# Row maxima moved by ScalarE from PSUM into the query stack, the first layer's mask added by TensorE, and two phases in a new order

## What is computed

```python
logits = q @ k.T * scale            # per head: 512 x 512; the first layer adds a Fourier bias
logits = where(causal, logits, -inf)
attn = softmax(logits)              # exp(logits - row maximum) / sum
out = attn @ v
```

## Time and profile before

| | us |
|---|---|
| median of three runs | 4009.02 |
| the profiled execution, its own time | 3993.08 |
| its span in the profile | 3991.3 |
| PE busy | 3393.3 (85%) |
| DVE busy | 2720.8 (68%) |
| ACT busy | 2003.3 (50%) |
| POOL busy | 1021.1 (26%) |
| mean granted clock of TensorE | 0.923 |

### The profile page before, as it was taken

How to read it: one execution, slowest core, us unless ns; L and a number is a source line. 1 busy time by engine, 2 the same in 40 slices (tenths; PEclk the granted TensorE clock), 3 DMA queues, 4 the chain that set the end, 5 groups by cost and what they waited for, 6 DMA issues and landing times.

```text
span 3991.3 us, 58259 instructions
## 1 busy us (share of the span) xinstructions
PE 3393.3 (85%) x19406; PEld 2516.8 (63%) x19406; DVE 2720.8 (68%) x8320; ACT 2003.3 (50%) x3683; POOL 1021.1 (26%) x1554
## 2 busy tenths in 40 slices
PE   2798888888888874789999999999999884799998
PEld 1566666666666652567777777777777653566665
DVE  5577777877877754356666667766666653588886
ACT  3355555555555542234444444444444443477776
POOL 1133433333433332112222222222222210000000
PEclk8899999999999986899999999999999976799999
DMA  6444444344444302134444444444444432000010
GB/s 180 68 84 85 74 77 80 76 91 80 75 76 79 63 16 74 32 74 70 84 86 86 85 86 85 84 82 84 82 84 86 75 70 85 1 32 32 32 32 22
DMA packets 207497, 284.23 MB, mean 71 GB/s; under 512 B 50977, under 2 KB 135970, under 8 KB 198370
## 3 DMA queue, kind: packets, MB, share of 16 engines
q1 hardware_dynamic: 207202, 280.52, 35.3%
HBM read 179.49 MB, written 96.73 MB: 69 GB/s over the span
## 4 chain that ended last, share of the span: by engine, by line
PE 63%; DMA 13%; DVE 9%; ACT 6%; issue 4%; POOL 3%; SPq 2%; POOLq 0%; ACTq 0%; DVEq 0%
PE ps L812 34%; DMA q_stack<-nmaxT 11%; PE ps L960 8%; PE ps L939 6%; PE ps L1158 5%; PE ps L974 4%; ACT pt L1623 2%; PE ps L914 2%; POOL pt L1812 1%; PE ps L985 1%; SPq L1937 1%; DVE ps L1304 1%; PE ps L1034 1%; DVE bn L1333 1%; DVE x_ring L1330 1%
## 5 line engine op out<-in xcount | busy, mean ns | idle before, releaser
L1304 DVE CUSTOM_DVE_ANT_0 ps<-ps,future 128x512 f32<-128x512 f32 (+3 forms) x2048 | 958.5, 514 | 335.4 <-PE ps L939 328.6
L1623 ACT ACTIVATE pt<-ps 128x512 f32<-128x512 f32 x1280 | 719.7, 597 | 513.4 <-PE ps L960 499.9
L960 PE MATMUL ps<-q_stack,k_stack 97*128 97x512 f32 (+3 forms) x2048 | 563.6, 355 | 214.7 <-DMA q_stack<-nmaxT 181.9
L1812 POOL TENSOR_SCALAR_AFFINE_SELECT pt<-pt 128x256 f32<-128x256 f32 x1024 | 404.9, 432 | 731.0 <-ACT pt L1623 730.8
L960 PEld LDWEIGHTS ps<-q_stack,k_stack 97*128 97x128 f32 x2048 | 365.7, 200 | 352.5 <-DMA q_stack<-nmaxT 214.2
L939 PE MATMUL ps<-k_stack,q_stack 96*128 96x512 f32 (+3 forms) x2048 | 540.0, 347 | 52.0 <-DVE nmax L1304 33.4
L939 PEld LDWEIGHTS ps<-k_stack,q_stack 96*128 96x128 f32 x2048 | 374.4, 203 | 130.4 <-issue 44.9
L974 PE MATMUL ps<-pt,v_ones 128*32 128x512 f32 (+3 forms) x4096 | 331.2, 468 | 34.0 <-POOL pt L1812 34.0
L1818 POOL TENSOR_TENSOR rs<-rs,mhalf 128x4 f32<-128x4 f32 x96 | 97.2, 1013 | 1024.7 <-DVE rs L1340 1024.7
L1834 POOL TENSOR_TENSOR hid<-hid,gate_of 128x512 f32<-128x512 f32 x128 | 164.3, 1283 | 690.4 <-DVE hid L1444 690.4
L812 PE MATMUL ps<-eh,w_hi 128*128 128x512 f32 (+1 forms) x672 | 282.1, 420 | 13.9 <-DVE xl L1285 11.4
(11 more groups left out here) (268 smaller groups left out, 7438.9 us busy)
## 6 DMA issues: line engine op xcount, KB each, us to landing
qk_scratch<-parts SPq DMA_DIRECT2D x64, 1024.0 KB, 5.5
q_stack<-qk_scratch SPq DMA_DIRECT2D x384, 128.0 KB, 5.0
k_stack<-qk_scratch SPq DMA_DIRECT2D x384, 128.0 KB, 5.7
gate_of<-gate_scratch SPq DMA_DIRECT2D x128, 256.0 KB, 5.0
x_mid<-x_ring SPq DMA_DIRECT2D x32, 512.0 KB, 2.6
x_ring<-x_mid SPq DMA_DIRECT2D x32, 512.0 KB, 4.9
x_ring<-in_x SPq DMA_DIRECT2D x16, 512.0 KB, 4.6
out_dram<-x_ring SPq DMA_DIRECT2D x16, 512.0 KB, 3.0
```

The costliest lines, as they stand in the source:

```text
L960: done = e.matmul(bank(bank_of[piece])[:, at:at + SEQ - j * P], a.k[0:97, base + h, j * P:(j + 1) * P], a.q[0:97, base + h, j * P:SEQ], st ...
L1304: done = e.tensor_tensor_reduce(src, src, future[:, SEQ - width:SEQ], -1.0, 3e38, ALU.add, ALU.min, nmax[:, g % 2, u // 5 * 2 + h, t:t + 1])
L1623: e.activation(dst, src, ACT.Exp).then_inc(exp_up.sem)
L1812: done = e.affine_select(out=blk, in_=blk, compare_op=ALU.is_ge, fill=0.0, base=0, pattern=[[0, 2], [1, P]], channel_multiplier=-1)
```

## The change

1. `N` is four transposes instead of one: one for each tile of 128 queries, of the 128x4 maxima of the four heads, side by side in the same bank as 4x512.
2. ScalarE's copy to `nmaxT`, `nmaxT` itself and the DMA `mr` are gone. ScalarE has pieces `mr` instead, two for each group, one for two heads each: two activations copy the bank's 4x512 into rows 96 to 99 of `q_stack` at the head's place, with scale -1 in the first layer.
3. Rows 96 to 99 of `k_stack` hold, for head h of a group, a one in row 96+h and zeros in the others. `T` runs over 100 rows and picks its head's row by that. `T`'s units 0 and 5 wait for the copies of their half.
4. `N`'s bank is left when the second `mr` is done (`leaves`).
5. First layer only: VectorE's custom instruction gives way to a plain maximum (`tensor_reduce`) without mask and negation, one for each product and one for both products of unit 4 and 9 of a group, 14 a group. The mask is added before by TensorE: behind each of the 16 score products one more product, bf16, identity 128x128 times the diagonal block of `future`, 128 columns, into the same place. The second layer keeps the custom instruction.
6. GpSimd's fill of row 96 becomes copies of the identity's corner into rows 96 to 99, in both prologues.
7. The due times of phases 1 and 2 are all new (period 74.24 to 71.3 in phase 1, 91.43 kept in phase 2), and with them the order on every engine. Phase 3's table is unchanged.

```diff
 TABLE = {
-    1: (74.24, {
+    1: (71.3, {
...
             put("N", n, g)
-            put("mr", n, g)
+            put("mr", n, g, 0)
+            put("mr", n, g, 1)
...
+            if kind == "N":
+                return max_row[key + (1,)], "scalar", ("mr",) + key + (1,)
...
                         done = e.matmul(bank(bank_of[piece])[:, at:at + width],
                                         a.q[0:96, base + h, t * P:(t + 1) * P], a.k[0:96, base + h, 0:width],
-                                        start=True, stop=True)
+                                        start=True, stop=a.layer == 1)
+                        if a.layer == 0:
+                            done = e.matmul(bank(bank_of[piece])[:, at + t * P:at + width], ident_b[:, :],
+                                            future[:, SEQ - P:SEQ], start=False, stop=True)
...
-                    e.transpose(bank(bank_of[piece])[0:GROUP * TT, 0:P], a.nmax[:, g % 2].rearrange("p h t -> p (h t)"),
-                                ident[:, :]).then_inc(nmax_up.sem)
+                    for t in range(TT):
+                        done = e.transpose(bank(bank_of[piece])[0:GROUP, t * P:(t + 1) * P], a.nmax[:, g % 2, :, t],
+                                           ident[:, :])
+                    done.then_inc(nmax_up.sem)
...
-                    if u == 0:
-                        e.wait_ge(*max_row[g % 2][n, g])
+                    if u % 5 == 0:
+                        e.wait_ge(*max_row[n, g, u // 5])
...
-                                        a.k[0:97, base + h, j * P:(j + 1) * P], a.q[0:97, base + h, j * P:SEQ],
+                                        a.k[0:100, base + h, j * P:(j + 1) * P], a.q[0:100, base + h, j * P:SEQ],
...
+                    if n < BATCH:
+                        first = u // 5 * 2
+                        if u % 5 == 4:
+                            done = e.tensor_reduce(nmax[:, g % 2, first:first + 2, 1],
+                                                   bank(bank_of[piece]).rearrange("p (h k) -> p h k", h=2), AX.X, ALU.max)
+                        else:
+                            for h, t, at in SCORES[u % 5]:
+                                done = e.tensor_reduce(nmax[:, g % 2, first + h, t:t + 1],
+                                                       bank(bank_of[piece])[:, at:at + (t + 1) * P], AX.X, ALU.max)
+                        done.then_inc(max_up.sem)
+                        continue
...
-                elif kind == "N":
-                    n, g = key
-                    before = group_before(n, g, 1)
-                    if before:
-                        e.wait_ge(*max_row[1 - g % 2][before])
-                    e.wait_ge(*nmax_up[key])
-                    e.activation(att[n // BATCH].nmaxT[:, :], bank(bank_of[piece])[0:GROUP * TT, 0:P],
-                                 ACT.Copy).then_inc(nmax_copy.sem)
+                elif kind == "mr":
+                    n, g, half = key
+                    a = att[n // BATCH]
+                    base = (g % a.sets) * GROUP + 2 * half
+                    if half == 0:
+                        e.wait_ge(*nmax_up[n, g])
+                    for h in range(2):
+                        done = e.activation(a.q[96:100, base + h, :], bank(bank_of["N", n, g])[0:GROUP, :], ACT.Copy,
+                                            scale=-1.0 if n < BATCH else 1.0)
+                    done.then_inc(max_row.sem)
...
-                    e.memset(att[1].k[96:97, :, :].bitcast(F32), 1.0).then_inc(consts.sem)
+                    for k in range(att[1].sets):
+                        done = e.tensor_copy(att[1].k[96:100, GROUP * k:GROUP * (k + 1), :],
+                                             ident[0:GROUP, 0:GROUP].unsqueeze(2).broadcast_to([GROUP, GROUP, SEQ]))
+                    done.then_inc(consts.sem)
...
-                elif kind == "mr":
-                    n, g = key
-                    a = att[n // BATCH]
-                    base = (g % a.sets) * GROUP
-                    e.wait_ge(*nmax_copy[key])
-                    e.dma_start(a.q[96:97, base:base + GROUP, :].bitcast(F32).rearrange("p h (t q) -> p (h t) q", q=P),
-                                a.nmaxT[:, :].bitcast(F32)).then_inc(max_row[g % 2].sem, 16)
```

More of the change, by code:

```diff
@@ L207 @@
         "tensor": {
[25 rows of a table removed]
[25 rows of a table added]
         },
         "scalar": {
[19 rows of a table removed]
[19 rows of a table added]
         },
         "vector": {
[18 rows of a table removed]
[18 rows of a table added]
         },
         "gpsimd": {
[L276 to L280 removed]
+            "tb a1": [109.964],
+            "sel": [174.864, 175.546, 199.792, 201.389, 219.762, 232.016, 237.916, 239.691],
+            "ln a1": [294.319],
+            "h2": [None, None, -7.976, -6.958, 16.952, 16.972, 31.626, 31.785, 50.869, 54.144],
+            "ln ex": [62.607],
         },
         "sync": {
[L283 to L289 removed]
+            "ld 2": [-62.816],
+            "send": [97.351, 123.314],
+            "rows": [130.177, 147.541, 172.69, 197.914],
+            "st 2": [298.553],
+            "gh": [-29.334],
+            "sg": [-26.197, -20.337, -14.651, -7.854, 6.912, 11.241, 26.456, 39.232],
         },
@@ L493, in decoder @@
         s_up, max_up = signal("s_up", "tensor", "S"), signal("max_up", "vector", "S")
-        nmax_up, nmax_copy = signal("nmax_up", "tensor", "N"), signal("nmax_copy", "scalar", "N")
-        max_row = [signal(f"max_row{k}", "sync", "mr", 1, 16, lambda key, k=k: key[1] % 2 == k) for k in range(2)]
+        nmax_up, max_row = signal("nmax_up", "tensor", "N"), signal("max_row", "scalar", "mr")
         t_up, exp_up = signal("t_up", "tensor", "T"), signal("exp_up", "scalar", "T")
@@ L670, in buffers @@
                 self.nmax = sb(stack, f"nmax{layer}", [P, 2, GROUP, TT])
-                self.nmaxT = sb(stack, f"nmaxT{layer}", [GROUP * TT, P], F32R)
                 self.oT = sb(stack, f"oT{layer}", [P, SEQ])
@@ L1781, in gpsimd @@
                                     pattern=[[-1, P]], channel_multiplier=1).then_inc(consts.sem)
+                    e.wait_ge(consts.sem, 7)
+                    for k in range(att[0].sets):
+                        done = e.tensor_copy(att[0].k[96:100, GROUP * k:GROUP * (k + 1), :],
+                                             ident[0:GROUP, 0:GROUP].unsqueeze(2).broadcast_to([GROUP, GROUP, SEQ]))
+                    done.then_inc(consts.sem)
+                    e.wait_ge(consts.sem, CONST_READY)
                 elif kind == "prologue" and key[0] == 2:
```

50 lines of the change are left out of this document (21 added, 29 removed), and 236 rows, old and new, of the table TABLE.

## The result

The changed kernel takes **3679.32 us**, the median of four runs (3674.18 to 3684.48), against 4007.77 (4005.38 to 4009.14) for the kernel before on the same chip: a ratio of **0.918**, 95% interval 0.9165 to 0.9197. The profiled execution took 3679.51 with a span of 3677.7. The forecast was 3879 with a range from 3760 to 3970: faster, as said, but by 328 us instead of 130, outside the range and beyond even the first rival's 3764.

The account below looks back on a forecast made before the run. TensorE's work and waits, mostly for the nmaxT DMA, bound the kernel; batches of 83.6 us (1.7 less) and 95.8 (6.4 less), sixteen each, save 130 from 3993.1, giving 3863, plus 15.9 to the median: 3879 us, range 3760 to 3970.

Parts of the forecast that it names:

- the first rival: Phase 1 gains more, with masks at 3.8, idle 3 and clock 0.5 us a batch: 3764 us; chance 0.17.
- The new order itself: New due times of phases 1 and 2: costed at nothing beyond the other terms, its gain lying in the same waits.
- The DMA goes: TensorE's wait for the nmaxT DMA: -5.1 us a batch in phase 1, -6.4 in phase 2; 1.0 for late copies.
- ScalarE's load: Four copies for one on ScalarE: +2.1 us a group, +8.5 a batch, staying off the bound.
- `N`: Four transposes instead of one on TensorE: +1.3 us a batch in both phases, on the path.
- The mask products: 64 a batch on TensorE in phase 1, 0.06 to 0.12 us each: 6.7 us a batch, ends 3.8 and 7.7.
- VectorE's maxima: Plain maxima in phase 1 save VectorE some 3 us a batch, ends 0 and 9; 1 counted on the path.
- Idle time in phase 1: TensorE's idle time other than the DMA's goes from 6.8 to 5.0 us a batch.
- The clock in phase 1: Of 4.3 us a batch lost to the lower clock, 2.8 comes back and 1.5 stays for short waits.
- Phase 2: Period of 95.8 us a batch, 6.4 less: work 92.0, N 1.3, idle 0.7, late copies 1.0, clock 0.8.
- The second: Rival: phase 1 gains nothing, masks costing 7.7 us a batch and filling no wait: 3972 us; chance 0.19.
- The third: Rival: ScalarE takes the DMA's place, TensorE waiting for its copies and the held score bank: 4158 us; chance 0.07.

Follow-up runs that it names:

- e1: Changed kernel with the old orders in phases 1 and 2; ScalarE's copies and the mask products stay: 3920.36 us, ratio 0.982 to the kernel before.
- e5: Kernel before with ScalarE's copies for the DMA alone; old orders, mask on VectorE: 3909.6 us.
- e7: Kernel before with the new orders alone, the row maxima's DMA placed earlier in SyncE's queue than in e2: 3882.88 us, ratio 0.970.
- e4: Changed kernel without the mask products, plain maximum over masked keys too, so part of the computation is left out: 3622.73 us, ratio 0.907.
- e3: Changed kernel with the first layer's mask and maximum back on VectorE's custom instruction; new orders and ScalarE's copies stay: 3639.5 us, ratio 0.910.
- e8: Changed kernel with every ScalarE copy of the maxima done twice, first into rows nothing reads: 3884.5 us, ratio 0.970 to the kernel before.
- e2: Kernel before with the new orders alone; DMA for the row maxima and VectorE's mask kept: 4140.6 us, ratio 1.037.
- e6: Kernel before with the mask products alone; old orders and DMA for the row maxima kept: 4057.9 us.
- e10: e1 with N moved from the two score banks to the banks of other pieces: 3961.12 us, ratio 0.989 to the kernel before.
- e17: e13 with the second long stretch of T, seven products in the fourth group, broken up too: 3901.37 us, ratio 0.976 to the kernel before.
- e12: e3 with phase 2's first two score units of the third group moved later: 3640.11 us, ratio 0.908 to the kernel before.
- e13: e1 with phase 1's stretch of ten T products broken up by units of S on TensorE: 3900.84 us, ratio 0.973 to the kernel before.
- e16: Changed kernel with O directly behind PV and ScalarE's oT moved forward, in two groups of phase 1: 3721.27 us, ratio 0.930 to the kernel before.
- e14: Changed kernel with seven T units put in one stretch in phase 1's third group on TensorE: 3762.14 us, ratio 0.939 to the kernel before.
- e11: Changed kernel with O directly behind PV on TensorE in three of four groups of phase 1: 3773.91 us, ratio 0.942 to the kernel before.

## Why the prediction was wrong

Right in its sign, in that the DMA's wait goes, and in the period of phase 2; wrong by 200 us in size. The failed step is the sentence **"The new order itself I cost at nothing beyond what is said above, since its gain lies in the same waits"**. The runs show in its place that the order is the largest part: e1, the change without it, takes 3920 against 3679, 8.3 us more a batch in phase 1 and 3.2 in phase 2, and e5 and e7 show that order and copies give 145 us together that neither gives alone. My 3879 was a forecast of a kernel near e1. In detail, against the profiled executions (3863 forecast, 3679.5 measured; the other 16 us of the miss are the median's distance to the profiled run, which had been 15.9 before and is nothing after):

- **The DMA goes** (right). No `T` waits for it or for a copy; I had 1.0 us a batch for copies that come late, and there are none in either phase. That holds with the new order only. With the old one and VectorE's mask the copies gain 3.8 and 2.3 us a batch (e5), where I had put 7.9 and 8.7 on the DMA and its clock, 1.0 of it to be lost to ScalarE and 1.3 to `N`.
- **ScalarE's load**: +6.9 and +7.4 us a batch against 8.5: four copies in a row take 2.02 us, not 4 x 0.60, since they overlap. That a copy over 4 partitions costs what one over 128 costs was right.
- **`N`**: 1.1 and 1.0 us a batch against 1.3. Right.
- **The mask products**: 4.7 us a batch against 6.7, 73 ns each against 105; inside my bounds (3.8 to 7.7), near the lower one. I had put the successor's weight load at its full price in 48 of 64 cases. 32 us in all. The Trainium skill ("TensorE: Matmul & The Clock Gate", Back-to-back issue gap) gives about 81 ns a product for a stream of 128-column ones, an estimate of 5.2 us a batch; e4's 73 ns lie below that too, nearer to it than to my 105.
- **VectorE's maxima**: 67.3 to 62.7 us a batch, 4.6 against the 3 I took. On the path that is worth 1.0 us a batch (e4 against e3), as much as I had counted; but the mask product that buys it costs 3.6, so e3, which takes neither, is the faster kernel.
- **Idle time in phase 1**: 0.6 us a batch against 5.0. This is the order, and with 70 us the largest term. I had read the three releasers of the earlier trace rows as fixtures of the work. e1 shows them with the old order (5.6 us idle) and the changed kernel without.
- **The clock in phase 1**: nothing lost against 1.5 us a batch, 24 us. I had kept it for the short waits. This isn't the order alone: e1 still has such waits, 5.6 us a batch, and ran only 0.8 us a batch at the lower level. e5, which has 7.7 us of them and no DMA to wait for, ran 5.7 us at it. Which of the waits pull the clock down stays open.
- **Work in phase 1 itself**: 1.3 us a batch less than 69.1 + 1.3 and the masks, 21 us: the waits hidden in busy time, which I took for work. Together with the masks, the idle time and the clock 16 x 9.2 = 147 us.
- **Phase 2**: 96.4 against 95.8, so 13 us too much was promised. Its parts: TensorE busy 94.2 for 93.3, idle 2.2 for 1.7, clock nothing for 0.8. e1 tells that this was luck in part: with the old order it would have been 99.7, as `S` waits there 2.5 us a batch for its rows of `k_stack` (1.1 with the new order) and `O` 1.4 for `oT` (nothing).
- **The phases' ends**: 16 x (11.0 + 5.6) = 266 us come from the periods, and the two phases gained 314. The other 48 lie in their first and last batches, where I counted no more than in the middle. In e1 there is nothing of it (41 + 31 us gained, 44 + 38 by periods), and e7, the new order with the DMA, has it as well (87 + 18 gained, 54 - 12 by periods), so it belongs to the order too.

The rivals: the first (phase 1 gains more) had the direction and was too small by 85 us, with its idle time at 3. The second did not happen: phase 1 gained 11.0 us a batch, and without the mask products the period falls by less than they keep TensorE busy, so they aren't paid for twice. The third did not happen, but e8 and e1 show its waits, one doubling of the copies or one other order away. *Slower* was possible in a way that I didn't name: e2 and e6.

## What to carry to other kernels

When a change comes with a new order of the work, price the order by itself: list all waits of the stage, the short ones too, ask which of them the order and which the work demands, and put the case that all go into the range. Run the factors apart and together: here the copies gave 98 us, the order 125, both 368, and the third part, the mask's product on the bounding engine, cost 32 to 40 that the sum hid. And where several engines wait for each other in turn, an experiment that removes one wait and gains nothing does not prove it harmless: here removing one gave nothing (e10, e17, e12; e10 even lost 41 us against e1) or 1.1 us a batch (e13), while adding one cost 2.8 to 6.2 (e16, e14, e11).

## What the runs showed of the hardware

- A wait can hide in TensorE's busy time: the same products were busy for 77.0 us a batch in e1 and 73.8 after, with a clock of 1.00 in both (0.8 us a batch at the lower level in e1).
- A 128-column bf16 product with its own weights among fp32r products kept TensorE busy for 73 ns on average (e4 against the changed kernel).
- ScalarE's copy of 4x512 from PSUM takes 574 ns, four in a row 2.02 us, and one of 128x512 takes 598: 4 partitions cost nearly as much as 128.
- The DMA of 8 KB from `nmaxT` landed 1.8 us after its issue at best, and at worst 12.9 us in the kernel before, 11.4 in e2 and 9.3 in e7. TensorE waited for it for up to 13.6 us in e2 and 8.3 in e7; these two differ only in its place in SyncE's queue.
- The clock does not follow the sum of the waits: e14, with 2.7 us of idle time a batch in phase 1, ran 5.3 us a batch at the lower level, e1 with 5.6 us only 0.8, and e11 with 5.7 us 0.8 too. In six of e14's nine batches the lower level began right behind the second or the third wait for exp of the stretch; in the other three the same waits (0.4, 0.3 and 0.5 us) stood there and the clock stayed at 1.00, so what decides it isn't shown.
